# Causal mask of layer 1's turned scores: from a product on TensorE to a select on GpSimd

## What is computed

```python
scores = jnp.einsum('bqhd,bkhd->bhqk', q, k) / jnp.sqrt(hd)
causal = jnp.tril(jnp.ones((S, S), bool))
scores = jnp.where(causal, scores, -1000000000.0)
a = jax.nn.softmax(scores, axis=-1)
out = jnp.einsum('bhqk,bkhd->bqhd', a, v)
```

## Time and profile before

| what | us |
|---|---|
| median of 3 runs (lowest, highest) | 1983.15 (1978.88, 1984.26) |
| profiled execution, its time | 1975.98 |
| profiled execution, its span | 1974.0 |
| PE busy | 1731.3 (88%) |
| DVE busy | 1447.3 (73%) |
| ACT busy | 1000.0 (51%) |
| POOL busy | 586.7 (30%) |

### The profile page before, as it was taken

How to read it: one execution, slowest core, us unless ns; L and a number is a source line. 1 busy time by engine, 2 the same in 40 slices (tenths; PEclk the granted TensorE clock), 3 DMA queues, 4 the chain that set the end, 5 groups by cost and what they waited for, 6 DMA issues and landing times.

```text
span 1974.0 us, 46459 instructions
## 1 busy us (share of the span) xinstructions
PE 1731.3 (88%) x17489; PEld 1157.3 (59%) x17489; DVE 1447.3 (73%) x4539; ACT 1000.0 (51%) x2018; POOL 586.7 (30%) x839
## 2 busy tenths in 40 slices
PE   3898898888958659989999999989999999988997
PEld 2677776776745436545655655655655555655455
DVE  6777877787651247887887887887887788787756
ACT  2554454545522236647646646646645645644642
POOL 3100111011114138635604613613623531530000
PEclk6999999999988779989999999999999999999999
DMA  4522122112008232122212213123122122121111
GB/s 120 179 74 61 34 66 79 57 39 63 8 10 276 58 99 72 53 78 80 75 59 90 67 56 107 50 73 101 43 72 79 62 76 76 69 68 61 50 33 50
DMA packets 109932, 144.30 MB, mean 73 GB/s; under 512 B 18752, under 2 KB 90880, under 8 KB 108432
## 3 DMA queue, kind: packets, MB, share of 16 engines
q1 hardware_dynamic: 76576, 113.28, 18.7%
q10 hardware_dynamic: 30128, 18.49, 3.3%
q0 software_dynamic: 3008, 9.57, 1.4%
HBM read 112.89 MB, written 28.15 MB: 71 GB/s over the span
## 4 chain that ended last, share of the span: by engine, by line
PE 51%; DVE 11%; issue 3%; ACT 2%; DMA 1%; SPq 1%; POOL 1%; ACTq 0%; DVEq 0%; POOLq 0%
PE ps L1955 10%; PE ps L1940 8%; PE ps L2096 5%; PE ps L2110 5%; PE ps L1994 5%; PE ps L2005 4%; PE ps L1965 3%; DVE ps L2184 2%; PE ps L1211 2%; PE ps L1220 1%; DVE l_XY L2184 1%; PE ps L2045 1%; PE ps L1967 1%; DVE l_xn L2222 1%; PE ps L2025 1%
## 5 line engine op out<-in xcount | busy, mean ns | idle before, releaser
L1759 POOL TENSOR_SCALAR l_XY<-l_XY,l_nmax 128x512 f32<-128x512 f32 x512 | 388.7, 768 | 224.6 <-DVE l_nmax L2184 216.4
L2184 DVE CUSTOM_DVE_ANT_0 l_XY<-ps,strips 128x512 f32<-128x512 f32 x512 | 341.1, 686 | 141.2 <-PE ps L1940 138.6
L1940 PE MATMUL ps<-l_stack 72*128 72x512 bf16 (+3 forms) x1024 | 351.1, 348 | 66.0 <-DVE l_nmax L2184 54.0
L1816 ACT ACTIVATE PT<-ps 128x512 f32<-128x512 f32 x512 | 305.3, 599 | 198.1 <-PE ps L1955 185.3
L1955 PE MATMUL ps<-ident,l_XY 128*128 128x128 f32 x2048 | 319.1, 279 | 3.7 <-POOL l_XY L1759 2.9
L1955 PEld LDWEIGHTS ps<-ident,l_XY 128*128 128x128 f32 x2048 | 240.5, 141 | 110.2 <-ACT PT L1816 45.1
L2184 DVE CUSTOM_DVE_ANT_0 ps<-ps,mask 128x384 f32<-128x384 f32 (+3 forms) x512 | 244.5, 504 | 27.0 <-PE ps L1940 24.6
L1940 PEld LDWEIGHTS ps<-l_stack 72*128 72x128 bf16 x1024 | 101.0, 99 | 148.2 <-DVE l_nmax L2184 84.3
L1965 PE MATMUL ps<-l_stack 75*128 75x256 bf16 (+3 forms) x512 | 155.2, 305 | 12.9 <-ACT PT_odd L1824 6.1
L1824 ACT ACTIVATE PT_even<-ps 128x512 f32<-128x512 f32 (+1 forms) x256 | 120.5, 493 | 63.6 <-PE ps L1967 51.8
L2096 PE MATMUL ps<-l_fT,l_w_e 128*128 128x512 f32 x256 | 145.1, 656 | 2.3 <-DVE h_tok L2383 1.2
(11 more groups left out here) (309 smaller groups left out, 2983.9 us busy)
## 6 DMA issues: line engine op xcount, KB each, us to landing
l_stack<-parts_dram SPq DMA_DIRECT2D x384, 96.0 KB
stack<-parts_dram SPq DMA_DIRECT2D x48, 384.0 KB
l_w_e<-in_L_ffn_w_dram ACTq DMA_DIRECT2D x128, 128.0 KB
strips<-bias_dram SPq DMA_DIRECT2D x8, 1792.0 KB, 7.0
parts_dram<-l_parts SPq DMA_DIRECT2D x32, 384.0 KB, 2.5
parts_dram<-parts SPq DMA_DIRECT2D x16, 384.0 KB, 6.8
strips<-bias_dram POOLq DMA_DIRECT2D x12, 448.0 KB, 10.0
w_e<-in_L_ffn_w_dram SPq DMA_DIRECT2D x12, 256.0 KB, 6.1
```

What stands on the lines that cost most here:

```text
L1759: nc.gpsimd.tensor_scalar(XY[:, c % XY_BUFS], XY[:, c % XY_BUFS], -1.0, nmax[:, c % 8:c % 8 + 1], ALU.mult, ALU.add).then_inc(y_pool, 1)
L1816: nc.scalar.activation(PT[:, quad(u, r), j], src.rearrange("p (k q) -> p k q", q=P), ACT.Exp).then_inc(moved, 1)
L1940: nc.tensor.matmul(ps[:, n % 3, 0:w], stack[0:STACK, 0, h, q * P:(q + 1) * P], stack[0:STACK, 1, h, 0:w], start=True, stop=True).then_inc( ...
L2184: nc.vector.tensor_tensor_reduce(out=dst, in0=src, in1=add, scale=-1.0, scalar=3.0e38, op0=ALU.add, op1=ALU.min, accum_out=low).then_inc(s ...
```

## The change

The product with `mask_turned` is left out, and with it the tile and the two POOL instructions that prepared it. POOL instead zeroes the forbidden weights of a whole unit behind the exponential: one affine_select over the first 128 queries of the four heads, 128 partitions x 4 x 128 elements, in place. It stands in POOL's step 4u + 30, behind the shift of a kind 0 tile and ahead of everything else in that step. It waits until ACT has moved the unit's last tile, and raises `masked`. PE's product with the values waits for `masked` in place of `moved` and comes one step later (`W_AT` = 33).

```diff
-V_AT, W_AT = 13, 32
+V_AT, W_AT = 13, 33
...
-        mask_turned = sb("mask_turned", [P, P], BF16)
...
+        masked = sem("masked")
...
-                link(nc.gpsimd.memset(mask_turned[:], 0.0))
-                link(nc.gpsimd.affine_select(out=mask_turned[:], in_=mask_turned[:], compare_op=ALU.is_ge, fill=-BIG, base=0,
-                                             pattern=[[1, P]], channel_multiplier=-1))
...
+                def causal(u):
+
+                    wait_moved(pool, ("T", 4 * u + 3))
+                    late = turned_keys(u % 4)[:, :, 0:P]
+                    nc.gpsimd.affine_select(out=late, in_=late, compare_op=ALU.is_ge, fill=0.0, base=0,
+                                            pattern=[[0, 4], [1, P]], channel_multiplier=-1).then_inc(masked, 1)
...
                     if m >= 1 and m - 1 < ALL and kind((m - 1) // TILES) == 0:
                         shift(m - 1)
+                    u, r = divmod(m - B_LAG - 4, 4)
+                    if r == 0 and 0 <= u < ALL // 4 and kind(u // 16) == 1:
+                        causal(u)
                     for k in group_at(m, (m + 1, GROUP)):
                         split_max(k)
...
                     nc.tensor.matmul(ps[:, to, 0:T - k * P], stack[:, 1, h, k * P:(k + 1) * P], stack[:, 0, h, k * P:T],
-                                     start=True, stop=False)
-                    nc.tensor.matmul(ps[:, to, 0:P], ident_b[:], mask_turned[:], start=False, stop=True).then_inc(turned, 1)
+                                     start=True, stop=True).then_inc(turned, 1)
...
-                    wait_moved(pe, ("T", 4 * u + 3))
+                    pe.wait_ge(masked, 16 * earlier(s) + u % 16 + 1)
```

More of the change, by code:

```diff
@@ L1800, in _ @@
                 experts.scalar(act)
-                act.wait_ge(l1_pool, 11)
+                act.wait_ge(l1_pool, 9)
                 act.wait_ge(l1_loaded, 16 * 11)
@@ L1929, in _ @@
                 pe.wait_ge(l1_loaded, 16 * 11)
-                pe.wait_ge(l1_pool, 11)
+                pe.wait_ge(l1_pool, 9)
                 def scores(n):
@@ L2136, in _ @@
                 experts.vector(dve)
-                dve.wait_ge(l1_pool, 11)
+                dve.wait_ge(l1_pool, 9)
                 dve.wait_ge(l1_loaded, 16 * 11)
```

## The result

The changed kernel takes 1989.23 us (median of 20 runs, 1981.3 to 1998.96) against 1981.89 us (20 runs, 1978.88 to 1987.32): ratio 1.004, 95% interval [1.0027, 1.0053]. That is 7.3 us slower, where 8.4 us faster was forecast. The profiled execution took 1987.23 us, with a span of 1984.8.

What follows compares the result with a forecast made beforehand. PE was taken to set the pace where kind 1 tiles are turned. -19.0 + 1.0 + 9.6 = -8.4 us: profiled 1975.98 to 1967.6 us, median 1983.15 to 1974.8 us; range 1962 to 1986 us.

Steps and rivals of the forecast that it cites:

- The lump of the values: PE in overlaps: both kinds' values fall in one step, 18 times; +1.0 us, between nothing and 11.2 us.
- Term 1: PE, turned scores: dropping the 512 mask products gives -19.0 us, between -30.7 and -14.3.
- the 3 us taken off: PE's waits for ACT: part of the product's 22.0 us saving lost to longer waits; 3 us, between none and 7.7.
- the product was covered: PE saves 0.06 us each time, then waits for ACT or DVE; half the product's gain left; 1984.3 us, chance 0.15.
- the prediction's own sign for it: Profile after: the forecast is wrong if PE's waits for ACT grow by more than 8 us.
- Term 3: POOL, six overlaps' ends: last select delays the power DVE needs by 1.6 us; +9.6 us, from nothing to 15.6.
- The select itself on POOL: nothing: POOL beside PE's work: 128 selects of 0.61 us, 79 us of POOL, fit into its room and cost nothing.
- The rival of DVE and POOL in each other's way: Selects slow DVE's SBUF work by 0.44 us; with one in three, +18.6 us, 1993.4 us; chance 0.05.

Runs made afterwards that it cites:

- W: The kernel before with the values product one step later (W_AT 33 for 32), mask product kept, no select: 1979.52 us, ratio 1.0032.
- P: The kernel before with the mask product left out and no select in its place, W_AT 32: 1961.99 us, ratio 0.9941.
- S: The selects on POOL; run as the changed kernel with mask product put back, 1986.6 us, ratio 1.0082 to the kernel before.
- the run made for it: Version with W_AT 32 and the select behind the powers, mask product kept for slot 2's 64 tiles: 1975.61 us, ratio 0.9964 to the kernel before.

## Why the prediction was wrong

The kinds of cost that the prediction named were there. Two of its three terms had the wrong size, both on the same side, and each rests on a step that failed.

- **The lump of the values: +1.0 forecast, +6.3 to +8.9 measured.** This step failed most: "The work is the same and only its order differs, so I take +1.0". It weighed the lump only in the overlaps. There W costs nothing: the overlap is 0.4 to 1.1 us shorter with it. The cost is beside the experts, 6.6 to 11.5 us in every pair of profiles, where the values had been the filler of PE's wait for DVE's `h_tok` (some 4 us of it). PE's busy share of 45.79 in 47 us was read as "PE sets the pace"; it didn't show that a wait stood right behind the work. Slot 2 adds to it in two of four pairs. The prediction's upper end, 11.2 us, did hold the value, for another reason: that is luck.
- **Term 1, the product: -19.0 forecast, -11.6 measured.** The step that failed is "the chain's 22.0 us leave out what already stood beside such a wait", and the 3 us taken off on its strength. The waits at PE were not fixed in number or length. Those of the turned scores for ACT went from 82 to 126 and grew by 17.3 us, because a PE that arrives earlier meets ACT still at work where it had come just in time, and the scores' waits for DVE grew by 13.5 us. Part of the miss is of another kind: slot 2 grew by 3.0 us at a lower clock in the profile, where the forecast had it shrink by some 2.4 (64 of 512 products). How much of the 7.4 us is which isn't settled. The rival "the product was covered", at -9.5 us, was nearer for this term, and the prediction's own sign for it, waits for ACT grown by more than 8 us, showed. The value lay outside the stated ends, -30.7 and -14.3.
- **Term 3, the power behind the select: +9.6 forecast.** It was right in place, in cause and in count. For the old place of the values it was right in size too: with W_AT 32 DVE waits 1.51 us where 1.6 was forecast, and the selects cost 10.4 us in the six overlaps. In the changed kernel it is 1.07 us of waiting and 1.05 on the path, 6.3 us. The difference is W. The sum took the end of the unit's last exponential from the kernel before, 1.06 us behind the start of the power (1088.89 and 1087.83). With W alone and no select it ends only 0.36 us behind (1091.12 and 1090.76 in the rows above): 0.70 us less to wait for. All selects together cost 9.9 us, which agrees with 9.6 by chance: 6.3 us are the term, and the rest, 3.6 us, isn't traced to a place.
- **"The select itself on POOL: nothing"** held for PE: 0.63 us each, PE's values waited for it twice, and PE's transposes waited 2.8 us in all for POOL's shifts, as against 2.9 before. With the power first it doesn't hold for DVE, as the next point tells. In the reading of the earlier trace rows the exponential of 1218.37 is called that of the tile before; it is the last tile's own, and the end that the sum uses is right.
- **The rival of DVE and POOL in each other's way** was given 0.05 with 18.6 us. It is true in kind and small. The prediction looked at line 2197, and the cost shows at the scalings: +0.46 us for a select of 0.63 us, +0.19 us for one of 0.29. The rule of the Trainium skill that spoke against the change (GPSIMD Engine Reference, Specifications) names DVE instructions with two SBUF inputs or in a 2-port mode; the first of these alone was carried over into the prediction. The scalings have one tensor in SBUF as their input, so by that rule they would have to run in such a mode; no row shows the mode.

With the measured sizes, W's taken on top of P, the prediction's own sum is -11.6 + 8.9 + 9.9 = +7.2 us, where the kernel came out at +7.3. The 15.7 us between forecast and result are then 7.4 us from the product, 7.9 from the values' place and 0.3 from the selects. That so little is left over is partly luck: each part has an interval of more than 2 us to either side, and the selects' was measured with the product kept.

**What stays open.** Runs with a lower granted clock are longer: over the kernel before's 23 and 18 runs by about 1.0 us for 0.001. Both sets of the changed kernel's runs have 0.938 on the mean, leaving out one run of 2002.45 us at 0.898, the kernel before's 0.946. By that slope some 8 to 9 us would go with the clock, as much as the whole loss. But the kernels whose PE waits more also have the lower clock, so this doesn't part cause from effect; the costs of W and S above hold whatever part of them passes through the clock. Why slot 2 is slow at W_AT 33, and with W_AT 32 in two of eight profiles, isn't settled; the run made for it speaks against the product as the cause. Nor is it settled why single overlaps lose 1.6 us at a lower clock. In seven of the nine a DMA issue of 1.15 to 1.43 us in ACT's queue (see below) stands 24 to 30 us ahead of the fall, but two have none, and most such issues are followed by no fall.

## What to carry to other kernels

Here the share of an instruction on the chain of waits (22.0 us) was nearly twice what its removal brought (11.6): take it as the most to hope for, ask at each place what comes next to last, and expect the waits just beside it to grow. When a step is moved, look at what it filled where it was, in every kind of stretch and not only where it lands; a step that "only changes its order" can be the filler of a wait for another engine. When two parts of a change are summed from rows of the old kernel, ask whether the one moves the times that the other was worked out from, as the values' place did with the power's wait. And in an engine that works in order, put a result that another engine waits for ahead of a long instruction that nobody is waiting for: with the old place kept, that exchange alone took this kernel from 0.14% slower than before to 0.3% faster.

## What the runs showed of the hardware

- POOL's select over 512 elements a partition in place takes 0.624 us at best, 0.634 at the median and 1.18 at most in the changed kernel, over 128 elements 0.282 and 0.292 us (best and median).
- Four DVE scalings of 128x128 f32 with one tensor in SBUF take 1.11 us with POOL idle, 1.67 to 1.72 us beside 1.1 us of POOL's shifts, 1.86 beside 1.3 us, and 2.18 to 2.21 us beside 1.9 us of select and shifts: each microsecond of POOL's work beside them cost DVE 0.5 to 0.6 us.
- The bf16 product over 128 columns holds PE for 0.059 us from its start to the next one's at the median of 512, weights loaded each time.
- Mean granted TensorE clock over a kernel's runs: 0.949 with two mask products, 0.946 to 0.948 with one, 0.941 to 0.945 with none, and 0.938 to 0.943 with the selects in its place (without the one run at 0.898). It isn't PE's work alone that goes with it: with one product and the selects beside it the clock is 0.944.
- The DMA issues of the experts' weights in ACT's queue take 0.34 or 0.45 us as a rule, but now and then 0.9 to 2.1 us, up to four times in an execution, in the kernel before's second profile too. ACT's exponentials stand behind them: with W alone one of 1.60 us at 1024.79 held up the exponential of 1026.43. They blur differences of a microsecond between single profiles.
